# Four result banks in place of two in the expert stages, and the choice's exponential behind the first two gates

## The reference

```python
# L1 (and, with other sizes, L0 without the product with w3, and L2)
logits = xf @ gate_w.T
rw, sel = jax.lax.top_k(logits, TOP_K)                 # TOP_K = 2
rw = jax.nn.softmax(rw, axis=-1)
for e in range(E):
    we = jnp.sum(jnp.where(sel == e, rw, 0.0), axis=-1)
    h = jax.nn.silu(xf @ w1[e].T) * (xf @ w3[e].T)
    out = out + h @ w2[e].T * we[:, None]

# L3: sigmoid scores, the best 2 of 4 groups, then 4 of 16 experts, and a shared expert
scores = jax.nn.sigmoid(x2d @ router_weight.T)
h = jax.nn.silu(g) * u                                 # every expert, 64 wide
routed = jnp.einsum('te,teh->th', combine, yo)
return routed + shared
```

## Time and profile before

| what | value |
|---|---|
| median of three runs | 2603.59 us |
| the profiled execution | 2607.98 us |
| its span, first to last instruction | 2606.2 us |
| PE busy | 2113.5 us, 81% |
| DVE busy | 1558.3 us, 60% |
| ACT busy | 1176.4 us, 45% |
| POOL busy | 758.6 us, 29% |
| mean granted TensorE clock | 0.880 |

### The profile page before, as it was taken

How to read it: one execution, slowest core, us unless ns; L and a number is a source line. 1 busy time by engine, 2 the same in 40 slices (tenths; PEclk the granted TensorE clock), 3 DMA queues, 4 the chain that set the end, 5 groups by cost and what they waited for, 6 DMA issues and landing times. The chain is left out here.

```text
span 2606.2 us, 36968 instructions
## 1 busy us (share of the span) xinstructions
PE 2113.5 (81%) x12720; PEld 1272.8 (49%) x12720; DVE 1558.3 (60%) x3628; ACT 1176.4 (45%) x2304; POOL 758.6 (29%) x937
## 2 busy tenths in 40 slices
PE   7784995767848887997898888775999798677887
PEld 4572572225622224664454444472344466567555
DVE  4677337988848883554545555453557345655665
ACT  2443437654336664224667666432445322133344
POOL 0330004643331100002565556434443000153122
PEclk8796897988859998997999999885789898698899
DMA  1000000001032200002333222102220001000000
GB/s 37 37 1 6 1 1 6 1 1 53 1 111 49 45 1 1 1 1 90 80 79 82 71 79 59 50 1 67 48 51 3 1 1 68 28 1 1 1 1 17
DMA packets 38601, 80.35 MB, mean 31 GB/s; under 512 B 7344, under 2 KB 21680, under 8 KB 37392
## 3 DMA queue, kind: packets, MB, share of 16 engines
q1 hardware_dynamic: 35952, 75.00, 10.8%
q10 hardware_dynamic: 2464, 2.99, 0.4%
HBM read 51.75 MB, written 7.34 MB: 23 GB/s over the span
## 5 line engine op out<-in xcount | busy, mean ns | idle before, releaser
L731 ACT ACTIVATE spt<-P 128x1024 f32<-128x1024 f32 (+3 forms) x256 | 221.0, 863 | 195.3 <-PE P L585 195.3
L698 DVE TENSOR_REDUCE smf<-P 128x2 f32<-128x1024 f32 (+3 forms) x256 | 254.5, 1019 | 53.6 <-PE P L574 30.7
L2274 PEld LDWEIGHTS P<-W,e_h 128*128 128x128 f32 (+1 forms) x1952 | 219.6, 190 | 61.2 <-issue 52.3
L2274 PE MATMUL P<-W,e_h 128*128 128x128 f32 (+1 forms) x1952 | 226.2, 277 | 13.3 <-DVE X L2467 13.3
L2260 PE MATMUL P<-XT,W 128*128 128x512 f32 x424 | 223.6, 625 | 12.0 <-ACT e_g L2346 8.8
L1085 POOL TENSOR_TENSOR d_e<-d_e,d_rc 128x512 f32<-128x512 f32 (+3 forms) x256 | 180.0, 725 | 177.6 <-DVE d_rc L991 147.6
L2467 DVE SCALAR_TENSOR_TENSOR X<-P,WE,X 128x128 f32<-128x128 f32 x448 | 126.1, 344 | 147.6 <-PE P L2274 147.6
L1034 ACT ACTIVATE d_e<-d_e,d_mn 128x512 f32<-128x512 f32 (+3 forms) x256 | 141.7, 554 | 130.6 <-DVE d_mn L983 130.3
L2346 ACT ACTIVATE e_g<-P 128x512 f32<-128x512 f32 x148 | 88.1, 597 | 242.0 <-PE P L2260 238.2
L2365 DVE TENSOR_TENSOR e_h<-e_g,P 128x512 f32<-128x512 f32 x148 | 101.3, 685 | 111.2 <-PE P L2264 109.9
L2264 PE MATMUL P<-XT,W 128*128 128x512 f32 x296 | 155.8, 608 | 0.9 <-DVE e_h L2365 0.9
(11 more groups left out here) (407 smaller groups left out, 4197.2 us busy)
## 6 DMA issues: line engine op xcount, KB each, us to landing
d_bt<-in_alibi SPq DMA_DIRECT2D x32, 512.0 KB, 3.7
d_moved<-d_raw SPq DMA_DIRECT2D x256, 64.0 KB, 2.4
ska<-parts_k SPq DMA_DIRECT2D x72, 64.0 KB
sqa<-parts_q SPq DMA_DIRECT2D x72, 64.0 KB
W<-in_w_L_xattn SPq DMA_DIRECT2D x1, 4291.0 KB, 13.7
W<-in_w_L_ffn SPq DMA_DIRECT2D x1, 3333.0 KB, 11.0
W<-in_w_L_ffn SPq DMA_DIRECT2D x1, 3155.0 KB, 10.1
parts_k<-sparts SPq DMA_DIRECT2D x8, 384.0 KB, 2.5
```

Source lines behind the costliest of these rows:

```text
L698: v.tensor_reduce(MF[:, n % 2, u, :], P[:, bank:bank + 2, 0:wide(u)], AX.X, ALU.max, negate=True).then_inc(s("max"), 1)
L731: a.activation(PT[:, n % 3, :, t, N - late(t):N], P[:, BANK_T:BANK_T + 2, 0:late(t)], ACT.Exp, scale=SC).then_inc(s("exp"), 1)
L2274: last = pe.matmul(P[:, PY + j % 2, 128 * t:128 * (t + 1)], HT[rows, q % RING, blk, 128 * t:128 * (t + 1)], w2, start=n == 0, stop=n == le ...
```

## The change

Results go to bank 4 + j % 4, so that result j waits until result j - 4 has been taken, not j - 2. Result 2 is the first to use bank 6, where the logits lay; it waits until DVE has read them (`shifted`). Result 3 is the first in bank 7, which held the turned chunk 3. On ACT the exponential (or sigmoid) moves behind activations 0 and 1: it stands in front of activation 2, with its wait for `shifted`.

```diff
--- before.py
+++ after.py
@@ -2267,11 +2267,13 @@
                 pe.wait_ge(s("hidden") if gated else s("act"), n_up[q + 1])
                 for m, (_, parts) in enumerate(units[q % U][1]):
                     j = n_out[q] + m
-                    if j >= 2:
-                        taken(pe, j - 2)
+                    if j >= 4:
+                        taken(pe, j - 4)
+                    elif j == 2:
+                        pe.wait_ge(s("shifted"), 1)
                     for t in range(4):
                         for n, (blk, rows, w2) in enumerate(parts):
-                            last = pe.matmul(P[:, PY + j % 2, 128 * t:128 * (t + 1)], HT[rows, q % RING, blk, 128 * t:128 * (t + 1)], w2,
+                            last = pe.matmul(P[:, PY + j % 4, 128 * t:128 * (t + 1)], HT[rows, q % RING, blk, 128 * t:128 * (t + 1)], w2,
                                              start=n == 0, stop=n == len(parts) - 1)
                     last.then_inc(s("y"), 1)
 
@@ -2317,8 +2319,6 @@
             apply(2)
             apply(3)
             copy(2)
-            a.wait_ge(s("shifted"), 1)
-            a.activation(SCO[:], L[:], ACT.Sigmoid if mode == "groups" else ACT.Exp).then_inc(s("exp"), 1)
 
             def scaled(q):
 
@@ -2332,7 +2332,7 @@
                     a.wait_ge(s("sum2"), sums_before(n - 1))
                 for t in range(4):
                     dst = SUM2[:, c % 2, 128 * t:128 * (t + 1)] if q % U == 0 else SCALED[:, n % 2, 128 * t:128 * (t + 1)]
-                    last = a.activation(dst, P[:, PY + j % 2, 128 * t:128 * (t + 1)], ACT.Copy, scale=k.WE[:, 4 * c + t, units[q % U][1][1][0]:units[q % U][1][1][0] + 1])
+                    last = a.activation(dst, P[:, PY + j % 4, 128 * t:128 * (t + 1)], ACT.Copy, scale=k.WE[:, 4 * c + t, units[q % U][1][1][0]:units[q % U][1][1][0] + 1])
                 last.then_inc(s("scaled"), 1)
 
             for q in range(ALL_U):
@@ -2340,6 +2340,9 @@
                     slot_free(a, q)
                 for f in range(len(units[q % U][0])):
                     j = n_up[q] + f
+                    if j == 2:
+                        a.wait_ge(s("shifted"), 1)
+                        a.activation(SCO[:], L[:], ACT.Sigmoid if mode == "groups" else ACT.Exp).then_inc(s("exp"), 1)
                     a.wait_ge(s("gate"), j + 1)
                     if gated and j >= 2:
                         a.wait_ge(s("hidden"), j - 1)
@@ -2460,7 +2463,7 @@
                         v.wait_ge(s("added"), mine)
                     for t in range(4):
                         x = k.X[:, 4 * c + t, :]
-                        y = P[:, PY + j % 2, 128 * t:128 * (t + 1)]
+                        y = P[:, PY + j % 4, 128 * t:128 * (t + 1)]
                         if e is None:
                             last = v.tensor_tensor(x, x, y, ALU.add)
                         else:
```

## The result

The changed kernel took 2573.16 us (median of six runs, 2563.30 to 2590.22) against 2603.45 (six runs, 2597.24 to 2605.23): a ratio of 0.9894 with a 95% interval of 0.9856 to 0.9933. The profiled execution took 2583.49 us, its span is 2581.6, 24.6 less than before.

A forecast was written before the change was run, and what follows sets the result against it. TensorE, busy 2113.5 of 2606.2 us, was taken as the bound, its waits as the gain: 3.0 + 1.3 + 0.7 + 12.8 = 17.8 us, median 2603.59 - 17.8 = 2585.8 us, range 2579 to 2597.

The forecast's parts named there:

- The start of L0, L1 and L2: Expert stages' starts: first activations ahead of the exponential let block 2 start earlier, gaining 3.0, 1.3 and 0.7 us.
- The third table load: ACT at each expert stage's start: one more table load, 1.28 us, costed at nothing because ACT idles during the logits.
- within 0.05 us of the room in the other stages: Stages other than L3: with the skill page's drain, ACT's chain of 6.4 us would just about fill the room.
- L3's start: Start of L3's experts: no gain, since DVE has no gap and its hidden blocks pace TensorE.
- The banks in L3: L3's down products: four result banks remove TensorE's 13.3 us of waits, gaining 12.8 us; bounds 6 and 12.8.
- If the last stall goes: End of L3: the last pair's sum then waits for POOL; 0.5 us lost, so 13.3 - 0.5 = 12.8.
- its list: Signs expected in the trace after: L2467 waits gone, twelve table loads, activations 0 and 1 earlier, new up product 2 wait.
- no later stage of L3's ring took over: Rival in L3: scaled results, POOL's sums or hidden blocks come late, half of 13.3 us stays: 2592 us; chance 0.12.
- the clock came back behind the restart: Rival at the starts: clock rises no earlier, most of the 5.0 us is lost: 2590.8 us; chance 0.12.
- a clock that stays low: Slower rival in L1 to L3's choice: clock kept at 1.2 GHz, about 50 us lost, 2636 us; chance 0.03.

The follow-up runs named there:

- the reversed pairs: The changed kernel with the two experts of every odd pair in L3 in reversed order: 2578.42 us against 2599.92, ratio 0.9909.
- interleaved pairs: The changed kernel with a pair's two results made tile by tile in turn: 2554.30 us against 2602.09, ratio 0.9828.
- the second's: The changed kernel measured and traced once more, unaltered, against the kernel before: 2566.67 us against 2599.92, ratio 0.9882 (0.9859 to 0.9904).

## Why the prediction was wrong

**The start of L0, L1 and L2: right.** 3.0, 1.3 and 0.7 were forecast; at equal clock they are 3.3, 1.1 (186.1 against 187.2) and 0.7 (144.0 against 144.7). The chain worked as written: in L1 the next stop of TensorE behind the residual sum is still there, at 1023.10, and moved with DVE.

```profile
1013.04 0.68 DVE L2368 TENSOR_TENSOR e_h<-e_g,P 128x512 f32<-128x512 f32 x1
...
1013.77 2.07 PE L2264 MATMUL P<-XT,W 128*128 128x512 f32 x2 [0.79 <-DVE e_h L2368]
1013.80 1.28 ACT L2349 ACT_TABLE_LOAD   x1 [1.64 <-DVE e_h L2368]
...
1023.06 0.30 PEld L2264 LDWEIGHTS P<-XT,W 128*128 128x128 f32 x2 [0.63 <-DVE e_h L2368]
```

**The third table load: free, as costed.** The trace has twelve loads in the four stages, as forecast. The exponential's load ran at once and ended before the shifted logits in all four stages. The first load, the two activations and the next load follow each other in 1.30, 1.10 and 1.28 us (270.26, 271.56, 272.66 above), so the drain of some 1380 ns in the Trainium skill (ScalarE: Activation LUTs, "What ACT_TABLE_LOAD costs") isn't seen here either, while its 1283 ns for the load agree with every row. (The forecast's "within 0.05 us of the room in the other stages" holds for L1 and L2, where 6.38 and 6.42 us lie between the first load and the exponential; in L0 it is 6.68.) One detail differed: in the gated stages the function's second load came not behind the exponential but behind the wait for hidden block 0 (1013.80 above). It cost nothing, since TensorE was busy with up product 2.

**L3's start: nothing, right.** From the norm's root to the first down product it took 48.2 us before and after. Up product 2 waits 3.9 us there, up from 0.7.

**The banks in L3: the step that failed.** "If the last stall goes [...] 13.3 - 0.5 = 12.8" priced the waits and took the busy time of TensorE as given, with 12.8 as the upper bound. The runs show 19.75. The waits went as written, and the end gave back 0.6 (0.5 in the forecast): DVE's sum (L2477) now waits 0.62 us for POOL.

```profile
2570.48 0.88 DVE L2468 TENSOR_TENSOR X<-X,P 128x128 f32<-128x128 f32 x4 [0.52 <-PE P L2276]
...
2570.61 1.26 POOL L2542 TENSOR_TENSOR e_sum<-e_sum,e_scaled 128x512 f32<-128x512 f32 x1 [1.98 <-ACT e_scaled L2335]
...
2571.98 0.69 DVE L2477 TENSOR_TENSOR X<-X,e_sum 128x512 f32<-128x512 f32 x1 [0.62 <-POOL e_sum L2542]
```

No sign in its list asked for the busy time: the waits, the table loads and the order of ACT came as listed, and the sum was still 7.0 us short. What was missing is 12 x 0.58 = 7.0 us: each wait also kept the matmuls on rows 0 to 63 of the next unit from overlapping with those on rows 64 to 127 of the last one (0.34, shown by the reversed pairs), and made TensorE start anew (0.24, seen in the starts). The trace of before could have told it: of the 16 matmuls of a pair the next gate product comes 1.64 us after the first, 0.82 for each half, while the eight of a shared expert take 0.97 (2512.98 to the gate product at 2513.95), though an instruction of either kind is as long. The Trainium skill (TensorEngine Tiling (Array Packing), "Key Properties") says that tiles operate independently, so that different ones load weights and multiply in parallel; the starts 0.004 to 0.006 us apart, the reversed and the interleaved pairs bear it out for two halves of 64 rows.

**The rest of the median.** By the traces, the change is worth 19.75 + 3.3 + 1.1 + 0.7 = 24.9 us at equal clock, which lies within the interval of the first measurement (17 to 37 us) and at the edge of the second's (25 to 37). The forecast for the median was 12.6 us too high, 7.0 of it by the term above. A part of the other 5.6 is L3's second value before: 6.4 us in two of six traces, some 2 us in the mean. The rest is probably in how often an execution gets the higher clock. The twelve runs of the changed kernel lie in two groups: four at 2580 to 2590 us, and eight at 2563 to 2575. All three of its traces, with L2_ffn's attention at 280.5, lie where the four do; 2580 less the 14 us of that attention is 2566, an estimate, and that is where the eight lie. Of the 47 runs of the kernel before in these comparisons only two took less than 2592 us, and its one trace with the attention at 266.5 took 2589.71. The other edits show it too: the traces of the banks alone (2572.29) and of the move alone (2582.11) have 266.5, and four of six and five of twelve of their runs lie within 4 us of these times. So the median of the changed kernel is very likely helped by a clock that the kernel before seldom gets. The forecast had nothing for that, and why the share differs stays open: no run varies where the attention starts and nothing else.

**The rivals.** None of them came: no later stage of L3's ring took over, the clock came back behind the restart, and the slower case, a clock that stays low, didn't show. All rivals made the gain smaller; none was written for a gain above the waits.

## What to carry to other kernels

A removed wait is worth just its own length only if the instructions around it keep theirs: look at what would run next to each other when it is gone, above all matmuls that use different halves of the rows. Where two matmuls of 64 rows are independent, put them in turn: here it brought 13.4 us more than the banks, for no extra work (with two banks only 6.2 us, since the waits grew). And trace a kernel more than once before a gain of under 1% is booked by stage: two single traces would have given L0 twice what the edit is worth.

## What wasn't expected of the hardware

- Sixteen matmul instructions of 64 rows x 128 columns took 1.64 us, to the next gate product, in two runs of eight on different row halves, and 1.10 us in turn; 32 took 2.74 and 1.99. In turn, one of each row half started together: 0.006 to 0.007 us apart in a stretch without waits, 0.036 apart behind a wait.
- The clock of TensorE differed between executions of one program at the same place: 0.82 against 1.00 over 50 us of one attention stage, 14 us in its time, and 5.33 against 3.71 us for one stage's logits, 3.3 us in its time.
- A stop of TensorE that the profile reports as 0.76 us cost 1.0 ahead of matmuls on half rows, the overlap not counted, and 0.80 ahead of matmuls on full rows.
